# Expert stage of a GNN and mixture-of-experts kernel: four places for weights and results, beta moved to VectorE, first tile's loads reordered

## What is computed

```
gate_logits = x @ gate_w + gate_b
topk_vals, topk_idx = top_k(gate_logits, 2);  topk_w = softmax(topk_vals)
h = relu(x @ w1[e] + b1[e])               # 256 -> 512
expert_out = h @ w2[e] + b2[e]            # 512 -> 256
y = x + sum over the two of topk_w * expert_out
out = (y - mean) / sqrt(var + eps) * gamma + beta
```

## Time and profile before

| | |
|---|---|
| median of 3 runs | 1500.34 us (1492.19 to 1501.63) |
| the profiled execution | 1497.36 us |
| its span, first to last instruction | 1495.6 us, mean granted TensorE clock 0.957 |
| TensorE busy, matmul / weight load | 88% / 77% |
| VectorE, ScalarE, GpSimd busy | 72%, 60%, 17% |
| DMA over the span | 283.03 MB, mean 189 GB/s |
| expert stage, by the first and last of its instructions | about 1150 to 1438 us |

### The profile page before, as it was taken

How to read it: one execution, slowest core, us unless ns; L and a number is a source line. 1 busy time by engine, 2 the same in 40 slices (tenths; PEclk the granted TensorE clock), 3 DMA queues, 4 the chain that set the end, 5 groups by cost and what they waited for, 6 DMA issues and landing times. The chain is left out here.

```text
span 1495.6 us, 31303 instructions
## 1 busy us (share of the span) xinstructions
PE 1309.2 (88%) x9561; PEld 1158.1 (77%) x9562; DVE 1078.2 (72%) x1894; ACT 891.1 (60%) x1985; POOL 260.2 (17%) x232
## 2 busy tenths in 40 slices
PE   4587777777899999999999999999976899999985
PEld 1477777777778888888888888888853899998875
DVE  8988988887876655766655756655575798787847
ACT  1788987887855555555555545555341666666563
POOL 1300000000030000000000000000001688888720
PEclk9899999998999999999999999999986999999998
DMA  5388888888886666666666666666321778878763
GB/s 187 73 201 202 200 203 198 199 191 206 214 254 205 185 185 176 193 178 184 185 184 176 192 169 185 182 188 181 114 88 63 233 238 242 251 246 254 234 211 120
DMA packets 236493, 283.03 MB, mean 189 GB/s; under 512 B 16269, under 2 KB 173045, under 8 KB 236421
## 3 DMA queue, kind: packets, MB, share of 16 engines
q1 hardware_dynamic: 228741, 261.28, 63.2%
q0 software_dynamic: 7680, 20.98, 4.5%
HBM read 194.27 MB, written 87.93 MB: 189 GB/s over the span
## 5 line engine op out<-in xcount | busy, mean ns | idle before, releaser
L869 PE MATMUL ps_rows<-h_both,a_high 128*128 (+1 forms) x1875 | 505.3, 397 | 11.3 <-ACT halves L604 5.3
L696 DVE TENSOR_TENSOR a_low<-a_raw,a_high 128x640 fp32r<-128x640 f32 x375 | 305.6, 823 | 231.7 <-ACT a_high L590 228.7
L590 ACT ACTIVATE a_high<-a_raw 128x640 fp32r<-128x640 f32 x375 | 274.4, 740 | 288.6 <-PE ps_rows L872 266.7
L869 PEld LDWEIGHTS ps_rows<-h_both,a_high 128*128 128x128 f32 x1875 | 329.5, 190 | 69.8 <-ACT halves L604 14.4
L872 PEld LDWEIGHTS ps_rows<-h_both,a_low 128*128 128x128 f32 x1875 | 275.5, 190 | 32.7
L872 PE MATMUL ps_rows<-h_both,a_low 128*128 (+1 forms) x1875 | 284.2, 282 | 0.0
L834 PE MATMUL ps_w<-lo_hot,key_w 128*120 128x160 bf16 x2736 | 239.2, 248 | 35.7 <-DVE key_w L680 35.7
L834 PEld LDWEIGHTS ps_w<-lo_hot,key_w 128*120 128x120 bf16 x2736 | 225.7, 142 | 41.9 <-ACT key_w L563 34.9
L572 ACT ACTIVATE win<-ps_w 128x480 f32<-128x480 f32 x304 | 148.0, 570 | 53.4 <-PE ps_w L839 40.5
L680 DVE TENSOR_TENSOR key_w<-key_hot,tab_marks 128x1440 bf16<-128x1440 bf16 (+1 forms) x228 | 164.4, 776 | 0.0
L563 ACT ACTIVATE key_w<-key_hot,third_b 128x120 bf16<-128x120 bf16 x456 | 141.3, 418 | 5.4 <-DVE key_hot L671 3.0
(11 more groups left out here) (244 smaller groups left out, 1651.7 us busy)
## 6 DMA issues: line engine op xcount, KB each, us to landing
a_raw<-a_rows SPq DMA_DIRECT2D x375, 320.0 KB, 3.2
a_rows<-win SPq DMA_DIRECT2D x228, 240.0 KB, 3.6
w_raw<-in_L_ffn_w SPq DMA_DIRECT2D x80, 512.0 KB
a_rows<-win SPq DMA_DIRECT2D x76, 180.0 KB
b_t<-in_L_ffn_b SPq DMA_DIRECT2D x40, 128.0 KB
found<-results SPq DMA_DIRECT2D x6, 640.0 KB, 8.6
hf<-in_x SPq DMA_DIRECT2D x1, 3072.0 KB
x<-in_x SPq DMA_DIRECT2D x1, 3072.0 KB
```

Source lines behind the costliest of these rows:

```text
L590: a.activation(a_high[:, u, :], a_raw[:, u, :], ACT.Copy).then_inc(high_split, 1)
L696: v.tensor_tensor(a_low[:, u, :], a_raw[:, u, :], a_high[:, u, :].bitcast(F32), ALU.subtract).then_inc(low_split, 1)
L869: nc.tensor.matmul(ps[:, banks[w][r], :], a_high[:, u, r * P:(r + 1) * P], both, start=first, stop=False, skip_group_check=True)
```

## The change

It does five things:

1. `w_raw` and `w_loaded` have four places instead of two. The load for tile t waits for w_low of tile t-4 (`w_low_ready` at t-3). b2 is loaded three tiles behind the weights in SP's queue instead of one.
2. `y_t` and `y_stored` have four places instead of two; result(t) waits for the scatter of tile t-4.
3. GpSimd no longer adds beta. VectorE does, at its start of the last stage, in five instructions of five chunks each.
4. At the start, GpSimd issues gather(0) ahead of `ones` and the identity, and gather(1) ahead of `none`; SP holds w2 of tile 0, and so all that follows it, until the first tokens are in.
5. TensorE does first(0) ahead of turn(1).

```diff
-    y_t = sb("y_t", [P, 2, HALVES, D])
+    y_t = sb("y_t", [P, 4, HALVES, D])
-    w_raw = [sb(f"w{n}_raw", [P, 2, WN]) for n in (1, 2)]
+    w_raw = [sb(f"w{n}_raw", [P, 4, WN]) for n in (1, 2)]
+    B2_LATER = 3
...
-            if late(t, 2):
-                sp.wait_ge(w_low_ready[n], t - 1)
-            sp.dma_start(w_raw[n][:, u, :]...).then_inc(w_loaded[n][u], 16)
+            if late(t, QUEUE):
+                sp.wait_ge(w_low_ready[n], t - (QUEUE - 1))
+            sp.dma_start(w_raw[n][:, q, :]...).then_inc(w_loaded[n][q], 16)
...
         def run(t, q):
-            u = q % 2
             if there(t):
                 e = expert(t)
-                load(0, t, u, e)
-                load(1, t, u, e)
-            if there(t - 1):
-                load_b2(t - 1, 1 - u, expert(t - 1))
+                load(0, t, q, e)
+                if isinstance(t, int) and t == 0:
+                    sp.wait_ge(x_loaded[0], 16 * HALVES)
+                load(1, t, q, e)
+            if there(t - B2_LATER):
+                load_b2(t - B2_LATER, (q - B2_LATER) % 2, expert(t - B2_LATER))
...
-        g.memset(ones[:], 1.0).then_inc(tabs, 1)
-        g.memset(none[:], 0.0).then_inc(tabs, 1)
-        pool.wait_ge(tabs, 2)
-        g.affine_select(out=ident[:], in_=ones[:], ...).then_inc(tabs, 1)
...
-        for t in range(MT + 6):
+        gather(0)
+        g.memset(ones[:], 1.0).then_inc(tabs, 1)
+        pool.wait_ge(tabs, 1)
+        g.affine_select(out=ident[:], in_=ones[:], ...).then_inc(tabs, 1)
+        gather(1)
+        g.memset(none[:], 0.0).then_inc(tabs, 1)
+        for t in range(2, MT + 6):
             if t < MT:
                 gather(t)
             if t >= 6:
                 scatter(t - 6)
-            if 8 <= t < 8 + s.CH:
-                c = t - 8
-                if c == 0:
-                    pool.wait_ge(bt_in, 16)
-                g.tensor_tensor(x1[:, c, :], x1[:, c, :], bt[:], ALU.add).then_inc(x1_ready, 1)
...
-        def result(t, u):
+        def result(t, q):
+            u = q % 2
             dve.wait_ge(b2_loaded[u], nth(t, u))
             dve.wait_ge(second_done, t + 1)
-            if late(t, 2):
-                dve.wait_ge(y_stored[u], (nth(t, u) - 16) * HALVES)
+            if late(t, QUEUE):
+                dve.wait_ge(y_stored[q], (nth_weights(t, q) - 16) * HALVES)
...
         def run(t, q):                      # TensorE
             u = q % 2
+            if isinstance(t, int) and t == 0:
+                first(0, 0)
             if there(t + 1):
                 turn(t + 1, 1 - u, (q + 1) % QUEUE)
-            if there(t):
+            if there(t) and not (isinstance(t, int) and t == 0):
                 first(t, u)
...
         dve.wait_ge(gm_in, 16)              # VectorE, last stage; AT_ONCE = 5, CH = 25
-        dve.wait_ge(x1_ready, CH)
+        dve.wait_ge(bt_in, 16)
+        for c in range(0, CH, AT_ONCE):
+            cs = slice(c, c + AT_ONCE)
+            v.tensor_tensor(x1[:, cs, :], x1[:, cs, :], bt[:].unsqueeze(1).broadcast_to([P, AT_ONCE, D]),
+                            ALU.add).then_inc(x1_ready, 1)
+        dve.wait_ge(x1_ready, CH // AT_ONCE)
```

More of the change, by code:

```diff
@@ L1302, in phase_experts @@
     x_loaded = [sem(f"tokens_in_{q}") for q in range(QUEUE)]
-    y_stored = [sem(f"results_out_{u}") for u in range(2)]
-    w_loaded = [[sem(f"w{n}_in_{u}") for u in range(2)] for n in (1, 2)]
+    y_stored = [sem(f"results_out_{q}") for q in range(QUEUE)]
+    w_loaded = [[sem(f"w{n}_in_{q}") for q in range(QUEUE)] for n in (1, 2)]
     bt_in = sem("beta_in")
-    x1_ready = sem("x1_ready")
     b2_loaded = [sem(f"b2_in_{u}") for u in range(2)]
@@ L1340, in nth_token, with nth_weights @@
         return (t - q) * 8 + 16 * HALVES
+    def nth_weights(t, q):
+        return (t - q) * 4 + 16
     def iterations(eng, last, run):
@@ L1360, in expert, with load @@
             return bass.DynSlice(sp.value_load(routes.expert[0:1, one(t)], min_val=0, max_val=s.E - 1), 1)
-        def load(n, t, u, e):
+        def load(n, t, q, e):
             dram = (w1, w2)[n]
-            if late(t, 2):
-                sp.wait_ge(w_low_ready[n], t - 1)
-            sp.dma_start(w_raw[n][:, u, :].rearrange("p (k f) -> p k f", f=dram.shape[2]),
-                         dram[e, :, :].rearrange("a (k p) f -> p (a k) f", p=P)).then_inc(w_loaded[n][u], 16)
+            if late(t, QUEUE):
+                sp.wait_ge(w_low_ready[n], t - (QUEUE - 1))
+            sp.dma_start(w_raw[n][:, q, :].rearrange("p (k f) -> p k f", f=dram.shape[2]),
+                         dram[e, :, :].rearrange("a (k p) f -> p (a k) f", p=P)).then_inc(w_loaded[n][q], 16)
         def load_b2(t, u, e):
@@ L1390, in _ @@
                 run(j * 4 + q, q)
-        run(MT, MT % QUEUE)
+        for t in range(MT, MT + B2_LATER):
+            run(t, t % QUEUE)
     @block.gpsimd
@@ L1417, in scatter @@
                         ap=routes.row[:, t * HALVES + h:t * HALVES + h + 1], axis=0),
-                    in_=y_t[:, t % 2, h, :], in_offset=None,
-                ).then_inc(y_stored[t % 2], 16)
-        for t in range(MT + 6):
+                    in_=y_t[:, t % QUEUE, h, :], in_offset=None,
+                ).then_inc(y_stored[t % QUEUE], 16)
+        gather(0)
+        g.memset(ones[:], 1.0).then_inc(tabs, 1)
+        pool.wait_ge(tabs, 1)
+        g.affine_select(out=ident[:], in_=ones[:], pattern=[[1, P]], compare_op=ALU.is_equal,
+                        fill=0.0, base=0, channel_multiplier=-1).then_inc(tabs, 1)
+        gather(1)
+        g.memset(none[:], 0.0).then_inc(tabs, 1)
+        for t in range(2, MT + 6):
             if t < MT:
@@ L1434, in _, with weights @@
         a = nc.scalar
-        def weights(n, t, u):
-            act.wait_ge(w_loaded[n][u], nth(t, u))
+        def weights(n, t, q):
+            act.wait_ge(w_loaded[n][q], nth_weights(t, q))
             if late(t, 2):
                 act.wait_ge((first_done, second_done)[n], t - 1)
-            a.activation(w_high[n][:, u, :], w_raw[n][:, u, :], ACT.Copy).then_inc(w_high_ready[n], 1)
+            a.activation(w_high[n][:, q % 2, :], w_raw[n][:, q, :], ACT.Copy).then_inc(w_high_ready[n], 1)
         def tokens(t, u):
@@ L1462, in run @@
             if there(t):
-                weights(1, t, u)
+                weights(1, t, q)
             if there(t + 1):
-                weights(0, t + 1, 1 - u)
+                weights(0, t + 1, (q + 1) % QUEUE)
                 tokens(t + 1, 1 - u)
@@ L1477, in _, with weights @@
         v = nc.vector
-        def weights(n, t, u):
+        def weights(n, t, q):
+            u = q % 2
             dve.wait_ge(w_high_ready[n], t + 1)
-            v.tensor_tensor(w_low[n][:, u, :], w_raw[n][:, u, :], w_high[n][:, u, :].bitcast(F32),
+            v.tensor_tensor(w_low[n][:, u, :], w_raw[n][:, q, :], w_high[n][:, u, :].bitcast(F32),
                             ALU.subtract).then_inc(w_low_ready[n], 1)
@@ L1497, in hidden @@
                             ALU.subtract).then_inc(hid_low_ready, 1)
-        def result(t, u):
+        def result(t, q):
+            u = q % 2
             dve.wait_ge(b2_loaded[u], nth(t, u))
             dve.wait_ge(second_done, t + 1)
-            if late(t, 2):
-                dve.wait_ge(y_stored[u], (nth(t, u) - 16) * HALVES)
+            if late(t, QUEUE):
+                dve.wait_ge(y_stored[q], (nth_weights(t, q) - 16) * HALVES)
             for h in range(HALVES):
-                v.tensor_tensor(y_t[:, u, h, :], ps_o[:, u, h, :], b2_t[:, u, :], ALU.add).then_inc(y_ready, 1)
+                v.tensor_tensor(y_t[:, q, h, :], ps_o[:, u, h, :], b2_t[:, u, :], ALU.add).then_inc(y_ready, 1)
         def run(t, q):
@@ L1516, in run @@
             if there(t - 1):
-                result(t - 1, 1 - u)
+                result(t - 1, (q - 1) % QUEUE)
         weights(0, 0, 0)
@@ L1586, in _, with phase_combine @@
             run(t, t % QUEUE)
-    return x1_ready, tabs, ident, none, diag, gm, y_ready, y_stored
-def phase_combine(nc, s, ctx, block, routes, x1, y, gamma, moe_dram, out, x1_ready, tabs, ident, none, diag, gm, y_ready,
+    return tabs, ident, none, diag, gm, bt, bt_in, y_ready, y_stored
+def phase_combine(nc, s, ctx, block, routes, x1, y, gamma, moe_dram, out, tabs, ident, none, diag, gm, bt, bt_in, y_ready,
                   y_stored):
```

11 lines of the change are left out of this document (6 added, 5 removed).

## The result

The changed kernel takes 1475.01 us (median of 4 runs, 1470.76 to 1487.23) where the kernel before took 1496.98 us beside it (4 runs, 1492.19 to 1501.63). The ratio is 0.9849, 95% interval 0.9812 to 0.9886: 22 us or 1.5% faster. In two later comparisons the changed kernel itself came to 0.981 (e5) and the one with two result places, whose middle is the same, to 0.982 (e9). The forecast was 1475. That the median agrees with it to 0.01 us is luck: the four runs spread over 16 us, and the gain beside the kernel before was 22 us in this comparison and 29 in e5's, against 24.6 forecast.

A forecast was written before the change was run, and what follows sets the result against it. Bound: the expert stage, where GpSimd's queue and SP's weight loads hold TensorE back. Terms -22 (middle), -4 (start), +1.4 (last stage) sum to -24.6 us: 1472.8 from the profiled execution, 1475.7 from the median, stated as 1475; range 1467 to 1488.

The forecast's parts named there:

- main term: Expert stage, fourth turn to last: 36 periods fall from 6.81 to 6.2 us, -22 us; TensorE's floor is 6.144.
- weight loop: SP's queue: the b2 load waits for result(t-3), holding the next weights; 6.98 us a tile once additions are done.
- Freeing GpSimd alone would therefore return nothing: Expert stage: moving only the additions off GpSimd gains nothing, since the loop through SP's loads takes over.
- The 7.1 us of VectorE's wait go: Expert stage: with four result places, VectorE's 7.1 us of waiting for stored results disappears.
- the two loops: Expert stage: GpSimd's gathers, scatters and additions, and SP's b2 wait ahead of weights; both must go for any gain.
- GpSimd's 6.43 us a round: Expert stage: GpSimd without additions falls 0.29 us a tile behind TensorE, 9.7 us over 34 rounds, covered by slack.
- Rival A: Expert stage: GpSimd stays the bound; at 6.65 us a round the middle returns 6 us, total 1489 to 1492; chance 0.08.
- rival B: Expert stage: DMA transfers are the bound; period 6.6 us, middle returns 7.5 us, total 1487 to 1490; chance 0.07.
- the figure 309 for a full share: Expert stage's DMA: full bandwidth taken as 244 / 0.79 = 309 GB/s, against 277 GB/s needed.
- Start: -4: Expert stage's start, up to the fourth turn: earlier gather and first(0) gain 4 us, ends -1.2 and -6.
- Last stage: the term: Start of last stage: VectorE's additions lengthen the last two scatters, delaying result loads: +1.4 us, ends 0 and +7.6.
- Drain: Last turn to the last scatters: work and dependencies of tiles 37 to 39, unchanged, 0 us.

The follow-up runs named there:

- e5: The changed kernel run again without any edit: 1472.98 us, ratio 0.981 to the kernel before.
- e9: The changed kernel with two places for results instead of four, second run: 1473.67 us, ratio 0.982 to the kernel before.
- e10: The changed kernel with the 25 additions of beta back on GpSimd, second run: 1486.88 us, ratio 0.9895 to the kernel before.
- e2: The changed kernel with b2 loaded one tile behind the weights instead of three: 1491.7 us, ratio 0.9928 to the kernel before.
- e12: The changed kernel with b2 one tile behind the weights instead of three, second run: 1498.59 us, ratio 0.9969 to the kernel before.
- e4: The kernel before with only the additions moved from GpSimd to VectorE's start of the last stage: 1495.33 us, ratio 0.9941 to the kernel before.
- e7: The changed kernel with VectorE adding beta inside its expert-stage rounds, none in the last stage: 1471.54 us, ratio 0.98 to the kernel before.
- e6: The changed kernel with the old start (GpSimd's order, SP's token wait and first(0) ahead of turn(1) undone): ratio 0.9848 to the kernel before.
- e1: The changed kernel with the 25 additions of beta back on GpSimd, first run: 1500.8 us, ratio 0.9993 to the kernel before.
- e3: The changed kernel with two places for results instead of four, first run: 1497.76 us, ratio 0.9959 to the kernel before.
- e11: The changed kernel with beta added inside VectorE's rounds and eight matmuls on zeros in the last stage: 1469.04 us, ratio 0.9786 to the kernel before.

## Why the prediction was right, and where its steps were wrong

- **The sum and its main term held.** TensorE's floor of 6.144 was reached in all 36 periods, not 6.2: I had kept 2 us for stalls that did not come. e10 shows the additions' part, 14.5 us, in a run free of unnamed waits. e2 and e12 show that without the b2 order the weight loop stays, as argued, though not cleanly how much it costs. By profile the stage and what follows gained 25.87 us for 24.6 forecast. The range had a slip: its lower end, 1467, counts from the profiled execution; from the median, which the text names, it is 1470.
- **"Freeing GpSimd alone would therefore return nothing" was wrong.** e4 returns 10.2 us of the middle. I took the 6.98 of the last seven periods as the weight loop's own pace with a free GpSimd. With the additions gone throughout, the same loop ran at 6.53. In those seven periods GpSimd was not free yet: it was still back to back, working off what the additions had cost it, and VectorE still waited for stored results. The waits of the kernel before, 1371 to 1421 us:

```profile
DVE y_t L1505 <- DMA results<-y_t,r_row: 3.1, 2, 1.7
```

A stretch of seven periods was also too little to take a limit from. In the other direction e10 shows that the additions alone, kept, cost 14.5: the two loops overlap, and their parts do not add up to 24.
- **"The 7.1 us of VectorE's wait go": they went, but not by four places.** e9 with two has 0.6 us of it. That wait had been a consequence of GpSimd's lateness. The term was double-counted in words, not in the sum, since the middle was priced by its period.
- **GpSimd's 6.43 us a round was not its pace.** I had it fall behind by 9.7 us in 34 rounds. In the changed kernel its rounds are 6.14 on average over each four, single ones 5.64, though it waits for nobody: its gathers stay 5.9 to 6.4 us behind the turn that frees their place, from tile 8 to the last, and the lag does not grow. In e9 the same lag is a steady 7.7 to 7.9, in e7 9.5 to 10.1. An explanation, not tested: its issues lengthen by where they meet VectorE's instructions, VectorE goes in step with TensorE, and so GpSimd settles where a round of both fits. Rival A did not come true, but these runs do not show how far off it was.
- **Transfers (rival B) were no bound** at share 0.90 and 277 GB/s; the figure 309 for a full share was too low, as 399 GB/s at the start shows (and the 383 to 388 of the earlier trace rows had shown before).
- **Start: -4 was measured as -3.96,** by a larger gain at first(0) and 1.7 us given back: a gather of 7.06 us behind the prefetched weights, and a granted clock that rose to 1.00 only 2.6 us earlier (13.3 us into the stage instead of 15.9) while first(0) came 5.7 earlier. e6 prices the start at 4.6.
- **Last stage: the term was mis-sized, 3.35 for 1.4.** The scatter part was 1.31 as worked out (2.16 and 1.09 against 2 and 1.2 forecast). The missing 1.7 is mostly TensorE's clock after a longer wait: about 1.5, e6 against e5. A delay on TensorE's path can have this second price.
- **Drain:** -1.22 instead of 0. A wait for x_low after the last turn, from late weights, went with the others. I had called the drain pure work.

Open: the unnamed waits. e1, e2, e3, e4 (one comparison) and e12 (another chip) have them, by ScalarE 6 us in e4 to 41 in e3; e5 to e11 have none, e9 and e10 on the very chip of e1 to e4. The other nine runs of e3 are long too. In e3 TensorE's matmuls come up to 0.9 us apart for some microseconds, with the DMA share at 0.9 to 1.1. Loads of instructions by DMA are not the cause: the queues that carry them have 11 packets in this stage of e3 and 12 in e5's, and none from 1210 to 1350 us, where 19 of e3's periods lost 12.3 us. Whether it is something else in the core or outside it, no run here tells. The kernel before has 3.2 us of them from 1194 to 1358 us, so its 24 us of stalls need not be loops alone.

## What to carry to other kernels

More places in a buffer did not end the wait for what it holds (51 us in e2, 46 in e12) while another wait stood ahead of its loads in the same in-order queue: find what the issuing engine waits for next, and move that too. Before a row of waits is believed, compare the wait with the pause that this engine always has. Before an operation is moved to an idle engine, look at what that engine's neighbours do in that hole, since an instruction of one can lengthen another's (0.97 us became 2.16). And when a step is late by one microsecond ahead of TensorE, count the clock that it may lose as well.

## What the runs showed of the hardware that was not expected

- Indirect DMA issue on GpSimd against VectorE's two-input additions in SBUF: 2.16 us beside additions of 1.48 us each, 0.97 without them (changed kernel and e7).
- The clock after a wait is not a function of the wait alone: it fell after 2.20 us in the changed kernel and 2.21 in e2, and stayed at 1.00 through 2.48 us in e6.
- The core moved 399 GB/s for 2.5 us at the start and 386 in the last stage, with a DMA share above 1.0 in the profile's count.
- GpSimd, back to back and with no slack of its own in any row of waits, kept the period of the others, 6.14 us, at a lag that stayed the same, within 0.6 us, from tile to tile and differed from run to run (about 6 us in the changed kernel, 8 in e9, 10 in e7).
